# Attention on one core: q and k projected three groups ahead of their scores, the next row's normalisation moved by one step

## The chip, the cores and the metric

The kernel runs on one core of a Trainium2 chip. The metric is the device time of one execution in microseconds, the median of several runs. TensorE is called PE here, VectorE DVE, ScalarE ACT, GpSimd POOL, and SyncE, which issues all DMA transfers of this kernel, SP.

## The reference

Two layers are applied in turn to x (16 rows of the batch, 512 tokens, 512 features, float32). The change touches the first layer alone, up to its attention output y:

```python
xn = layer_norm(x, norm_w, norm_b)
q = (xn @ q_w + q_b).reshape(Bx, Tx, H, -1)
k = (xn @ k_w + k_b).reshape(Bx, Tx, H, -1)
att = jnp.einsum('bnhl,bmhl->bnmh', q, k)
att = att + (1.0 - mask) * -1000000.0
att = jax.nn.softmax(att, axis=2)
v = ((xn @ v_w + v_b) * src_mask[:, :, None]).reshape(Bx, Tx, H, -1)
y = jnp.einsum('bnmh,bmhl->bnhl', att, v).reshape(Bx, Tx, Dx)
```

There are 16 heads of 32 features. The rest of the first layer (a second normalisation, scale and shift from the conditioning vector, silu, output projection) and the whole second layer run in a second phase, which the change leaves as it is.

## The kernel before

The program has two phases, `attention_phase` and `projection_phase`, with a barrier between them. In the attention phase each of the five engines has its own instruction stream, and all order between engines is written out with semaphores.

**Groups and steps.** The 16 heads of a row of the batch are worked on in four groups (`g`, 0 to 3) of four heads. The program of every engine is a sequence of steps, one for each row `b` and group `g`, and each step has 16 slots (`k`, 0 to 15). Rows 1 to 14 run in a hardware loop, the first and the last are written out. In slot `k` of step (b, g) PE computes one exponential product (`exp_scores`, line 512) for the current group, three slots behind the step (`LAG = 3`), so slots 0 to 2 belong to the last three of the group before. In slots 0 to 10 it also computes one or two maximum products (`max_scores`, L497) for the next group, 16 in all (`maxima(k)`: slot 0 has score 0, slot 1 scores 1 and 2, slot 2 score 3, slot 3 scores 4 and 5, and so on). DVE reduces each (L862), which frees its bank; there are two banks, so score m waits until maximum m - 2 is done. In slot 12 the 16 columns of maxima are transposed (`transpose_max`, L503), DVE splits them into a high and a low part (L873, L875), and SP copies both as two rows, the shift, into `q_stack` (L325), where the exponential products of the next step need them from slot 3 on. ACT takes the exponentials (L728). PE multiplies probabilities and values after exponential products 6, 10, 14 and 2 of the next group (`weigh_values`, L523); POOL adds the probabilities of the four token tiles in three additions (`add_probs`, L271), and PE sums these after exponential product 7 of the next group (L537).

**Projections.** A projection of q, k or v is twelve products (L480) into one of two work banks, cut into four quarters of three products, each placed in a slot. `QUARTERS` names the slots: q in 0 to 3, k in 4 to 7, v tiles in 8 to 11 and 13 to 15. q and k are projected for the group two steps ahead. ACT writes the high part of the result to a staging buffer, one for q and one for k (L708), DVE the low part (L848), and SP copies them into `q_stack` and `k_stack` in three transfers each (`stack`, L318). The copies, with that of the mask rows (L310), count on one semaphore for each group, `stack_in`; PE waits for it before maximum product 0 of the group, ACT before it overwrites a staging buffer. v tiles 2 and 3 of a row are projected in step 0, tiles 0 and 1 of the next row in step 3.

**The next row.** x of row b + 1 is loaded in step 2 of the row before. Its statistics (`statistics_of_x`, L822 to L831) run on DVE in slot 13 of step 0, POOL then takes the inverse deviation (L431), and DVE normalises four tiles (L837) in slots 3 to 6 of step 1. PE transposes them in slots 8, 9, 11 and 13 (`X_TURNS`, L487), ACT and DVE write high and low parts (L702, L843), and from step 2 on the projections read the new row.

**Banks.** All uses of the two work banks are numbered in the order that `uses_of` gives, and `take_bank` makes PE wait until the use two before has been read:

```python
def take_bank(n):
    static, number = n
    if static >= 2:
        pe.wait_ge(work_read, number - 1)
    return work_bank[static % 2][:, :]
```

## Time and profile before

| | us |
|---|---|
| median of 3 runs (3141.38 to 3144.47) | 3141.91 |
| profiled execution, span on the core (no separate total of this execution is given) | 3140.1 |
| PE busy in it | 2820.6 (90%) |
| DVE, POOL, ACT busy | 1924.4, 1333.8, 1224.2 |
| attention phase, about | 1780 |

A busy share is a mean over both phases. The attention phase is the first 57% of the span and is told apart below by steps. The rows quoted later are from one row of the batch in the middle of the phase; the others repeat its pattern every 105.9 us. In the timelines a bracket behind a row is the idle time of that engine before it, and what ended it. "PEclk" is the share of full clock that TensorE was granted: 1.00 is 2.4 GHz, 0.50 is 1.2 GHz.

### The profile page before, as it was taken

To read this page: it belongs to the slowest core of one execution; us is meant where nothing else is said; L and a number is where in the kernel's file an instruction comes from. 1 tells how busy PE (TensorE), PEld (TensorE's weight loads), DVE (VectorE), ACT (ScalarE), POOL (GpSimd) and SP (SyncE) were. 2 spreads that over 40 slices of the span, in tenths; PEclk is the share of its full clock that TensorE was granted. 3 is DMA by queue.
4 is the path that set the end of the run, shared out by engine and by line. 5 is a ranking of instruction groups with operands and counts; after the bars stand their busy time and mean duration, and the time that the engine had idled before them with its cause. 6 is when DMAs were issued, how large, how long until landed. Compare 5 with 4: busy or idle time off the path is not lost. (4 is left out here: it accounts for less than half of the span.)

```text
span 3140.1 us, 43763 instructions
## 1 busy us (share of the span) xinstructions
PE 2820.6 (90%) x13890; PEld 1966.3 (63%) x13890; DVE 1924.4 (61%) x3292; ACT 1224.2 (39%) x2040; POOL 1333.8 (42%) x582
## 2 busy tenths in 40 slices
PE   6989899889988998899889789999999999999998
PEld 4555455555554555555455367777777777778876
DVE  5665666566556655665565466666666666666664
ACT  2444444444444444444444423332233333332232
POOL 0355555555555555545555333333333333333332
PEclk8999999999999999999999699999999999999999
DMA  7545454555455545545544311111101111111100
GB/s 209 93 68 85 81 85 69 85 85 85 72 85 85 85 72 85 85 72 85 85 72 72 118 48 45 44 40 44 37 34 40 40 44 44 44 42 32 43 28 27
DMA packets 114915, 211.44 MB, mean 67 GB/s; under 512 B 12408, under 2 KB 14508, under 8 KB 114876
## 3 DMA queue, kind: packets, MB, share of 16 engines
q1 hardware_dynamic: 114876, 210.94, 34.1%
q8 instruction: 22, 0.36, 0.0%
q14 instruction: 17, 0.14, 0.0%
HBM read 74.87 MB, written 34.18 MB: 35 GB/s over the span
## 5 line engine op out<-in xcount | busy, mean ns | idle before, releaser
L862 DVE TENSOR_REDUCE negmax<-max_bank 128x1 f32<-128x512 f32 x1024 | 682.6, 688 | 519.0 <-PE max_bank L497 518.6
L728 ACT ACTIVATE probs<-exp_bank 128x512 f32<-128x512 f32 x1024 | 598.3, 595 | 708.0 <-PE exp_bank L512 701.1
L271 POOL TENSOR_TENSOR probs_sum<-probs_sum,probs 128x2048 f32<-128x2048 f32 x126 | 577.4, 4582 | 224.6 <-ACT probs L728 222.8
L497 PE MATMUL max_bank<-k_stack,q_stack 98*128 98x512 f32 x1024 | 460.1, 454 | 127.1 <-DMA k_stack<-k_stage 87.8
L271 POOL TENSOR_TENSOR probs_sum<-probs 128x2048 f32<-128x2048 f32 x63 | 288.6, 4581 | 642.1 <-PE sums_bank L537 548.9
L497 PEld LDWEIGHTS max_bank<-k_stack,q_stack 98*128 98x128 f32 x1024 | 198.4, 195 | 426.7 <-issue 239.9
L512 PE MATMUL exp_bank<-q_stack,k_stack 100*128 100x512 f32 x1024 | 421.7, 423 | 23.6 <-ACT probs L728 23.3
L523 PE MATMUL y_bank<-probs,v_sb 128*32 128x512 f32 x2048 | 289.1, 638 | 0.7 <-ACT probs L728 0.7
L1487 POOL TENSOR_TENSOR sT_lo<-silu,sT_hi 128x512 fp32r<-128x512 f32 x128 | 168.1, 1324 | 238.8 <-DVE sT_hi L1602 238.8
L512 PEld LDWEIGHTS exp_bank<-q_stack,k_stack 100*128 100x128 f32 x1024 | 196.3, 195 | 109.0 <-ACT probs L728 71.8
L1269 PE MATMUL b_work<-ident,area 128*128 128x128 f32 x1536 | 195.6, 280 | 45.1 <-ACT silu L1427 18.8
L1269 PEld LDWEIGHTS b_work<-ident,area 128*128 128x128 f32 x1536 | 172.9, 144 | 65.3 <-ACT silu L1427 26.2
L1243 PE MATMUL b_work<-b_wout_hi,sT_hi 128*128 128x512 f32 x512 | 201.7, 394 | 9.6 <-issue 5.1
L1243 PE MATMUL b_work<-b_wout_lo,sT_hi 128*128 128x512 f32 x512 | 201.1, 393 | 0.0
L1243 PE MATMUL b_work<-b_wout_hi,sT_lo 128*128 128x512 f32 x512 | 201.0, 393 | 0.0
L1602 DVE CAST sT_hi<-silu 128x512 fp32r<-128x512 f32 x128 | 109.4, 865 | 113.1 <-ACT silu L1427 113.1
L1482 POOL TENSOR_TENSOR rstd_y<-var_eps_y,b_minus_half 128x4 f32<-128x4 f32 x32 | 32.7, 1022 | 322.3 <-DVE var_eps_y L1566 322.3
L1502 POOL TENSOR_TENSOR result<-area,row_out 128x512 f32<-128x512 f32 x64 | 82.7, 1294 | 181.3 <-DMA out_x<-result 181.3
L1427 ACT ACTIVATE silu<-b_work,film_b,film_a 128x512 f32<-128x512 f32 x128 | 93.0, 775 | 165.2 <-PE b_work L1269 154.3
L1243 PE MATMUL b_work<-b_wv_hi,x1T_hi 128*128 128x512 f32 x256 | 112.2, 438 | 49.7 <-ACT silu L1427 49.7
L1466 ACT ACTIVATE area<-area 128x512 f32<-128x512 f32 x64 | 40.5, 632 | 290.5 <-POOL area L1532 290.5
L1453 ACT ACTIVATE area<-area,kmax 128x512 f32<-128x512 f32 x64 | 46.3, 724 | 239.5 <-DVE kmax L1628 239.3
(203 smaller groups left out, 5397.3 us busy)
## 6 DMA issues: line engine op xcount, KB each, us to landing
q_stack<-q_stage SPq DMA_DIRECT2D x192, 256.0 KB
k_stack<-k_stage SPq DMA_DIRECT2D x192, 256.0 KB
x_sb<-in_x SPq DMA_DIRECT2D x16, 1024.0 KB, 5.4
yT_scratch<-y_stage SPq DMA_DIRECT2D x64, 256.0 KB
area<-yT_scratch SPq DMA_DIRECT2D x16, 1024.0 KB, 5.2
area<-in_x SPq DMA_DIRECT2D x64, 256.0 KB, 2.7
out_x<-result SPq DMA_DIRECT2D x64, 256.0 KB, 2.0
mask_bias<-mask_bias_scratch SPq DMA_DIRECT2D x16, 256.0 KB, 3.3
```

What stands on the lines that cost most here:

```text
L271: eng.tensor_tensor(probs_sum[:, :, :], so_far, probs[:, mt, :, :], ALU.add).then_inc(probs_added, 1)
L497: pe.matmul(max_bank[m % 2][:, :], q_stack[0:ROWS_MAX, g, j, nt * P:(nt + 1) * P], k_stack[0:ROWS_MAX, g, j, :], start=True, stop=True).th ...
L512: pe.matmul(exp_bank[k % 2][:, :], k_stack[0:ROWS_EXP, g, j, mt * P:(mt + 1) * P], q_stack[0:ROWS_EXP, g, j, :], start=True, stop=True).th ...
L523: last = pe.matmul(y_bank[DH0 * j:DH0 * (j + 1), :], v_sb[:, mt, P * j + DH0 * g:P * j + DH0 * (g + 1)], probs[:, mt, j, :], start=(mt == ...
L728: act.activation(probs[:, mt, j, :], exp_bank[k % 2][:, :], ACT.Exp).then_inc(exp_done, 1)
L862: dve.tensor_reduce(negmax[:, m:m + 1], max_bank[m % 2][:, :], AXX, ALU.max, negate=True).then_inc(max_done, 1)
L1243: last = pe.matmul(out, lhs(a, kt), rhs(c, kt), start=(kt == 0 and a + c == 0), stop=(kt == KT - 1 and a == 1))
L1269: last = pe.transpose(out[:, i * P:(i + 1) * P], src(i), ident[:, :])
L1427: act.activation(silu[:, kt % SILUS, :], bank(u), ACT.Silu, scale=film_columns(film_a[film], kt, row), bias=film_columns(film_b[film], kt, ...
L1487: pool.tensor_tensor(sT_lo[:, kt, :], silu[:, kt % SILUS, :], sT_hi[:, kt, :].bitcast(F32), ALU.subtract).then_inc(sT_lo_done, 1)
L1502: pool.tensor_tensor(result[:, tt, :], x_sb[:, tt, :], rows["out1"][:, :], ALU.add).then_inc(result_biased, 1)
L1602: dve.tensor_copy(sT_hi[:, kt, :], silu[:, kt % SILUS, :]).then_inc(sT_hi_done, 1)
```

## The change

q and k are projected three groups ahead (`AHEAD`). A table `TURNS` now gives each step its own slots: in step 0 v tiles 2 and 3 come first, then q and k; in step 1 the transposes of x come in slots 1, 3, 5, 7 and q and k in 8 to 15; in step 2 q lies in slots 4 to 7 and k in 8 to 11; step 3 is as before, but for the group after. The statistics of the next row move from slot 13 of step 0 to slot 2, the normalisation from slots 3 to 6 of step 1 to slots 9 to 12 of step 0. POOL takes the inverse deviation ahead of its first addition of step 0 instead of behind its second. q and k copies have a semaphore each, and SP issues its transfers in another order in steps 0 to 2. The prologue projects three groups of q and k instead of two. The reordering of `uses_of` follows from the table. The core of the diff:

```diff
@@ -205,34 +205,38 @@
...
+        AHEAD = 3
...
+        TURNS = [
...
+            {"v2": (0, 1, 2, 3), "v3": (4, 5, 6, 7), "q": (8, 9, 10, 11), "k": (13, 14, 15, 15)},
...
+        X_TURNS = (1, 3, 5, 7)
...
-        QUARTERS = {"q": (0, 1, 2, 3), "k": (4, 5, 6, 7), "v": (8, 9, 10, 11), "v'": (13, 14, 15, 15)}
...
-        X_TURNS = (8, 9, 11, 13)
...
@@ -356,31 +364,44 @@
             shift_rows(0, 0, FIRST_USES.index("m") + 1)
             def step(b, g, last=False, first=False):
-                if not last or g < NG - 2:
-                    s_b, s_g = (b, g + 2) if g + 2 < NG else (b + 1, g + 2 - NG)
-                    if not (first and g + 2 < NG):
-                        sp.wait_ge(exp_full, SLOTS * (step_of(b, g) - 1))
+                more = projects(g, last)
+                s_b, s_g = ahead(b, g, AHEAD)
+                def stack_of(n):
+                    sp.wait_ge(work_read, use(b, g, n, last)[1] + 1)
+                    stack(n, s_g)
+                def shift_of_next():
+                    if not last or g < NG - 1:
+                        shift_rows(*ahead(b, g, 1), use(b, g, "m", last)[1] + 1)
+                if more:
+                    if not (first and g == 0):
+                        sp.wait_ge(exp_full, SLOTS * step_of(b, g))
                     mask_rows(s_b, s_g)
                 if g == 2 and not last:
                     sp.wait_ge(work_full, use(b, 1, f"x{TT - 1}")[1] + 1)
                     if not (type(b) is int and b + 2 >= B):
                         load_x(b + 2)
-                if not last or g < NG - 2:
-                    sp.wait_ge(work_read, use(b, g, "q", last)[1] + 1)
-                    stack("q", s_g)
+                if more and g == NG - 1:
+                    stack_of("q")
                 if not (first and g == 0):
                     store_y(b, g - 1) if g else store_y(b - 1, NG - 1)
-                if not last or g < NG - 2:
-                    sp.wait_ge(work_read, use(b, g, "k", last)[1] + 1)
-                    stack("k", s_g)
+                if more and g >= 2:
+                    stack_of("q" if g == 2 else "k")
                 if g == 0 and not first:
                     store_sums(b - 1)
-                if not last or g < NG - 1:
-                    n_b, n_g = (b, g + 1) if g + 1 < NG else (b + 1, 0)
-                    shift_rows(n_b, n_g, use(b, g, "m", last)[1] + 1)
+                if g != 2:
+                    shift_of_next()
+                if more and g < 2:
+                    stack_of("q")
+                if more and g < NG - 1:
+                    stack_of("k")
+                if g == 2:
+                    shift_of_next()
             def load_x(b):
                 sp.dma_start(x_sb[:, :, :], x[b].rearrange("(t p) d -> p t d", p=P)).then_inc(x_in, DMA)
@@ -434,10 +455,10 @@
                 s = step_of(b, g)
                 if last and g == NG - 1:
                     return
+                if g == 0 and not last:
+                    inverse_deviation(b + 1)
                 add_probs(pool, s, 1, first)
                 add_probs(pool, s, 2)
-                if g == 0 and not last:
-                    inverse_deviation(b + 1)
                 add_probs(pool, s, 3)
             inverse_deviation(0)
@@ -491,7 +512,8 @@
                 j, nt = m // TT, m % TT
                 if m == 0:
-                    pe.wait_ge(stack_in[g], DMA * STACK_DMAS * (b + 1))
+                    for n in "qk":
+                        pe.wait_ge(stack_in[n][g], DMA * STACK_DMAS[n] * (b + 1))
                 if not (first and m < 2):
                     pe.wait_ge(max_done, SLOTS * step_of(b, g) + m - 1)
                 pe.matmul(max_bank[m % 2][:, :], q_stack[0:ROWS_MAX, g, j, nt * P:(nt + 1) * P],
@@ -655,24 +679,16 @@
                             max_scores(n_b, n_g, m)
                         if k == MAX_TURN:
                             transpose_max(n_b, n_g, use(b, g, "m", last))
-                    for name, slots in QUARTERS.items():
-                        if name in "qk":
-                            if last and g >= NG - 2:
-                                continue
-                            what, tile, u = name, (g + 2) % NG, name
-                        elif g == 0 or (g == NG - 1 and not last):
-                            tile = (2 if g == 0 else 0) + (name == "v'")
-                            what, u = "v", f"v{tile}"
-                        else:
-                            continue
+                    for name, slots in turns_of(g, last).items():
+                        what, tile = (name, (g + AHEAD) % NG) if name in "qk" else ("v", int(name[1]))
                         for kt in range(KT):
                             if slots[kt] != k:
                                 continue
-                            if name == "q" and kt == 0 and g == 2:
+                            if kt == 0:
+                                banks[name] = take_bank(use(b, g, name, last))
+                            if name == "q" and kt == 0 and g == 1:
                                 pe.wait_ge(work_read, use(b, 1, f"x{TT - 1}")[1] + 1)
-                            if kt == 0:
-                                banks[name] = take_bank(use(b, g, u, last))
                             project_quarter(what, tile, banks[name], kt, kt == 0, kt == KT - 1)
                     if g == 1 and not last and k in X_TURNS:
                         tt = X_TURNS.index(k)
@@ -759,10 +775,10 @@
             high_of_w("k")
             act.wait_ge(bias_done, 2)
             n = TT
-            for g in range(2):
+            for g in FIRST_GROUPS:
                 for what in "qk":
-                    if g == 1:
-                        act.wait_ge(stack_in[0], DMA * STACK_DMAS)
+                    if g:
+                        act.wait_ge(stack_in[what][g - 1], DMA * STACK_DMAS[what])
                     high_of(what, g, n, n)
                     n += 1
             copy_film(0)
@@ -987,37 +1005,43 @@
             HIGHS = 2 * NG + TT
-            def high_count(b, g, i):
-                return TT + 4 + HIGHS * b + (2 * g + (TT if g > 1 else 0)) + i + 1
+            def high_count(b, g, what):
+                before = 2 * g + (TT if g > 1 else 0)
+                at = ([f"x{tt}" for tt in range(TT)] if g == 1 else []) + ["q", "k"]
+                return TT + 2 * AHEAD + HIGHS * b + before + at.index(what) + 1
             def step(b, g, last=False):
                 has_next = not last or g < NG - 1
-                n_b, n_g = (b, g + 1) if g + 1 < NG else (b + 1, 0)
+                n_b, n_g = ahead(b, g, 1)
                 for k in range(SLOTS):
                     if has_next:
                         for m in maxima(k):
                             maximum(n_b, n_g, m)
-                    for i, what in enumerate("qk"):
-                        if k == QUARTERS[what][-1] + 1 and (not last or g < NG - 2):
-                            low_of(what, (g + 2) % NG, use(b, g, what, last)[0], high_count(b, g, i))
-                    if g == 1 and not last and 3 <= k < 3 + TT:
-                        normalise_x(b + 1, [k - 3])
+                    for what in "qk":
+                        if k == TURNS[g][what][-1] + 1 and projects(g, last):
+                            low_of(what, (g + AHEAD) % NG, use(b, g, what, last)[0], high_count(b, g, what))
+                    if g == 0 and not last and k == 2:
+                        statistics_of_x(b + 1)
+                    if g == 0 and not last and 9 <= k < 9 + TT:
+                        normalise_x(b + 1, [k - 9])
                     if g == 1 and not last and k - 1 in X_TURNS:
                         tt = X_TURNS.index(k - 1)
-                        low_of_x(tt, use(b, 1, f"x{tt}")[0], high_count(b, 1, 2 + tt))
-                    if k == 11 and (g == 0 or (g == NG - 1 and not last)):
-                        mt = 2 if g == 0 else 0
-                        add_value_bias(b if g == 0 else b + 1, mt, *use(b, g, f"v{mt}", last))
+                        low_of_x(tt, use(b, 1, f"x{tt}")[0], high_count(b, 1, f"x{tt}"))
+                    if g == 0 and k in (4, 8):
+                        mt = 2 if k == 4 else 3
+                        add_value_bias(b, mt, *use(b, 0, f"v{mt}", last))
+                    if g == NG - 1 and not last and k == 12:
+                        add_value_bias(b + 1, 0, *use(b, g, "v0"))
                     if has_next and k == MAX_TURN:
                         split_shift(n_b, n_g, *use(b, g, "m", last))
-                    if g == 0 and not last and k == 13:
-                        statistics_of_x(b + 1)
-                        if type(b) is int and b == 0:
-                            finish_film()
-                if g == 0 or (g == NG - 1 and not last):
-                    mt = 3 if g == 0 else 1
-                    add_value_bias(b if g == 0 else b + 1, mt, *use(b, g, f"v{mt}", last))
+                    if g == 0 and not last and k == 13 and type(b) is int and b == 0:
+                        finish_film()
+                for what in "qk":
+                    if TURNS[g][what][-1] == SLOTS - 1 and projects(g, last):
+                        low_of(what, (g + AHEAD) % NG, use(b, g, what, last)[0], high_count(b, g, what))
+                if g == NG - 1 and not last:
+                    add_value_bias(b + 1, 1, *use(b, g, "v1"))
             for g in range(NG):
                 step(0, g)
```

How the instructions move is shown at three places, from the written-out first row, whose order the loop repeats.

The first is DVE in step 0 of the first row, from its first reduces on, before (L857 adds the bias to a v tile, L822 to L831 are the statistics, L873 and L875 split the shift):

```order
L848 SCALAR_TENSOR_TENSOR q_stage<-work_bank,bias_cols,q_stage 128x512 [waits hi_done]
L862 TENSOR_REDUCE negmax<-max_bank 128x1 [waits max_full] x6
L848 SCALAR_TENSOR_TENSOR k_stage<-work_bank,bias_cols,k_stage 128x512 [waits hi_done]
L862 TENSOR_REDUCE negmax<-max_bank 128x1 [waits max_full] x3
L857 TENSOR_TENSOR v_sb<-work_bank,v_bias 128x512 [waits work_full]
L873 CAST shift<-work_bank 16x128 [waits shift_in0,work_full]
L875 TENSOR_TENSOR shift<-work_bank,shift 16x128 [waits shift_hi]
L822 BN_STATS stats<-x_sb 128x6 [waits x_in]
L822 BN_STATS stats<-x_sb 128x6 x3
L826 MEMSET var_eps 128x4 [waits ln_stats]
L828 BN_AGGR mv<-stats 128x2 x4
L831 TENSOR_TENSOR var_eps<-mv,var_eps 128x4 [waits ln_stats]
```

And the same place now:

```order
L879 TENSOR_REDUCE negmax<-max_bank 128x1 [waits max_full] x4
L839 BN_STATS stats<-x_sb 128x6 [waits x_in]
L839 BN_STATS stats<-x_sb 128x6 x3
L843 MEMSET var_eps 128x4 [waits ln_stats]
L845 BN_AGGR mv<-stats 128x2 x4
L848 TENSOR_TENSOR var_eps<-mv,var_eps 128x4 [waits ln_stats]
L879 TENSOR_REDUCE negmax<-max_bank 128x1 [waits max_full] x3
L874 TENSOR_TENSOR v_sb<-work_bank,v_bias 128x512 [waits work_full]
L879 TENSOR_REDUCE negmax<-max_bank 128x1 [waits max_full] x6
L874 TENSOR_TENSOR v_sb<-work_bank,v_bias 128x512 [waits work_full]
```

The statistics have moved from behind the last reduce to behind the fourth, with twelve reduces and both v tiles after them.

The second is the normalisation (L837) before, on DVE in step 1, behind the first six reduces:

```order
L862 TENSOR_REDUCE negmax<-max_bank 128x1 [waits max_full] x6
L837 TENSOR_SCALAR x_sb<-x_sb,mv,rstd 128x512 [waits rstd_done]
L862 TENSOR_REDUCE negmax<-max_bank 128x1 [waits max_full]
L848 SCALAR_TENSOR_TENSOR q_stage<-work_bank,bias_cols,q_stage 128x512 [waits hi_done]
L837 TENSOR_SCALAR x_sb<-x_sb,mv,rstd 128x512 [waits rstd_done]
L862 TENSOR_REDUCE negmax<-max_bank 128x1 [waits max_full] x2
L837 TENSOR_SCALAR x_sb<-x_sb,mv,rstd 128x512 [waits rstd_done]
L862 TENSOR_REDUCE negmax<-max_bank 128x1 [waits max_full]
```

And now, where it is L854, at the end of step 0:

```order
L879 TENSOR_REDUCE negmax<-max_bank 128x1 [waits max_full] x2
L854 TENSOR_SCALAR x_sb<-x_sb,mv,rstd 128x512 [waits rstd_done]
L879 TENSOR_REDUCE negmax<-max_bank 128x1 [waits max_full]
L854 TENSOR_SCALAR x_sb<-x_sb,mv,rstd 128x512 [waits rstd_done] x2
L865 SCALAR_TENSOR_TENSOR q_stage<-work_bank,bias_cols,q_stage 128x512 [waits hi_done]
L854 TENSOR_SCALAR x_sb<-x_sb,mv,rstd 128x512 [waits rstd_done]
L890 CAST shift<-work_bank 16x128 [waits shift_in0,work_full]
L892 TENSOR_TENSOR shift<-work_bank,shift 16x128 [waits shift_hi]
```

Three of the four tiles have moved ahead of, and one behind, the low part of q, and all four ahead of the shift.

The third is SP in step 2 before (mask rows, the load of x, q copies, the store of y, k copies, shift):

```order
L310 DMA k_stack<-mask_bias_scratch 2x4x512 [waits exp_full]
L386 DMA x_sb<-in_x 128x4x512 [waits work_full]
L318 DMA q_stack<-q_stage 32x4x512 [waits work_read]
L318 DMA q_stack<-q_stage 32x4x512 x2
L391 DMA yT_scratch<-y_stage 4x32x512 [waits y_read]
L318 DMA k_stack<-k_stage 32x4x512 [waits work_read]
L318 DMA k_stack<-k_stage 32x4x512 x2
L325 DMA q_stack<-shift 1x16x128 [waits work_read]
L325 DMA q_stack<-shift 1x16x128
```

And now:

```order
L318 DMA k_stack<-mask_bias_scratch 2x4x512 [waits exp_full]
L407 DMA x_sb<-in_x 128x4x512 [waits work_full]
L412 DMA yT_scratch<-y_stage 4x32x512 [waits y_read]
L326 DMA q_stack<-q_stage 32x4x512 [waits work_read]
L326 DMA q_stack<-q_stage 32x4x512 x2
L326 DMA k_stack<-k_stage 32x4x512 [waits work_read]
L326 DMA k_stack<-k_stage 32x4x512 x2
L333 DMA q_stack<-shift 1x16x128 [waits work_read]
L333 DMA q_stack<-shift 1x16x128
```

The store of y has moved ahead of the q copies; k copies and shift stand as before, while k itself is now finished four slots later.

## Rows read from the trace of the kernel before

**Rows 1.** Windows of steps 0 to 3: us, busy by engine, PEclk, DMA, GB/s.
```profile
724.60:749.50 24.90, 24.87 (x122) 15.69 (x122) 17.42 (x32) 12.72 (x22) 13.62 (x4) 1.00 0.50 76
...
749.50:777.40 27.90, 24.14 (x114) 13.44 (x113) 22.41 (x30) 13.51 (x24) 13.64 (x5) 0.94 0.44 67
...
777.40:803.60 26.20, 20.16 (x98) 11.00 (x97) 12.47 (x20) 11.58 (x20) 17.28 (x4) 0.95 0.59 112
...
803.60:830.50 26.90, 26.89 (x121) 16.18 (x121) 13.25 (x22) 11.32 (x19) 11.49 (x4) 0.93 0.46 69
```

**Rows 2.** Waits of PE, 698 to 804 us: in total, times, longest.
```profile
PE max_bank L497 <- DMA k_stack<-k_stage: 9.4, 3, 4.1
...
PE max_bank L497 <- DVE negmax L862: 2.3, 3, 1.0
...
PE exp_bank L512 <- ACT probs L728: 1.4, 3, 0.7
```

**Rows 3.** Timeline of PE, start and us: stalls in steps 1 and 3.
```profile
763.14 0.71 PE L497 MATMUL max_bank<-k_stack,q_stack 98*128 98x512 f32 x1 [0.98 <-DVE negmax L862]
...
803.61 0.79 PE L497 MATMUL max_bank<-k_stack,q_stack 98*128 98x512 f32 x1 [4.14 <-DMA k_stack<-k_stage]
```

**Rows 4.** SP's issues in step 2, and the landing time of the shift copies.
```profile
793.27 1.87 SPq L318 DMA_DIRECT2D k_stack<-k_stage  x3
...
797.01 1.21 SPq L325 DMA_DIRECT2D q_stack<-shift  x2
...
q_stack<-shift SPq DMA_DIRECT2D x2, 8.0 KB, 5.5
```

**Rows 5.** Timelines of DVE, POOL and PE, slots 2 to 4 of step 0.
```profile
728.47 1.29 DVE L862 TENSOR_REDUCE negmax<-max_bank 128x1 f32<-128x512 f32 x2 [0.24 <-PE max_bank L497]
...
729.46 4.61 POOL L271 TENSOR_TENSOR probs_sum<-probs_sum,probs 128x2048 f32<-128x2048 f32 x1 [1.99 <-ACT probs L728]
...
731.08 0.40 PE L497 MATMUL max_bank<-k_stack,q_stack 98*128 98x512 f32 x1
...
731.32 0.40 PE L480 MATMUL work_bank<-xT_hi,wk_hi 128*128 128x512 f32 x1
```

**Rows 6.** Statistics and normalisation before, with POOL's addition; var_eps as a group.
```profile
745.67 0.67 DVE L822 BATCH_NORM_STATS2 stats<-x_sb 128x6 f32<-128x512 f32 x1
...
748.58 4.02 DVE L831 TENSOR_TENSOR var_eps<-mv,var_eps 128x4 f32<-128x4 f32 x1
...
747.97 4.60 POOL L271 TENSOR_TENSOR probs_sum<-probs_sum,probs 128x2048 f32<-128x2048 f32 x1 [0.84 <-ACT probs L728]
...
758.08 2.70 DVE L837 TENSOR_SCALAR x_sb<-x_sb,mv,rstd 128x512 f32<-128x512 f32 x1
...
L831 DVE TENSOR_TENSOR var_eps<-mv,var_eps 128x4 f32<-128x4 f32 x14 | 56.2, 4018 | 0.5
```

**Rows 7.** POOL and PE in slots 10 to 13 of step 0.
```profile
742.52 4.61 POOL L271 TENSOR_TENSOR probs_sum<-probs 128x2048 f32<-128x2048 f32 x1 [8.45 <-PE sums_bank L537]
...
745.97 0.50 PE L480 MATMUL work_bank<-wv_hi,xT_hi 128*128 128x512 f32 x1
```

**Rows 8.** Groups of DVE, 200 to 1700 us: the reduces of the maxima.
```profile
L862 DVE TENSOR_REDUCE negmax<-max_bank 128x1 f32<-128x512 f32 x906 | 604.3, 688 | 455.4 <-PE max_bank L497 455.4
```

**Rows 9.** Timeline of PE where x is transposed in step 1.
```profile
768.37 1.06 PE L523 MATMUL y_bank<-probs,v_sb 128*32 128x512 f32 x8
...
769.36 0.50 PE L497 MATMUL max_bank<-k_stack,q_stack 98*128 98x512 f32 x1
...
769.70 0.60 PE L487 MATMUL work_bank<-ident,x_sb 128*128 128x128 f32 x4
...
770.06 0.48 PE L497 MATMUL max_bank<-k_stack,q_stack 98*128 98x512 f32 x1
```

**Rows 10.** Timeline of ACT in the prologue: the second group's q.
```profile
54.20 0.69 ACT L708 ACTIVATE q_stage<-work_bank,bias_cols 128x512 fp32r<-128x512 f32 x1 [15.35 <-DMA k_stack<-k_stage]
```

**Rows 11.** Window of step 2 of the last row, columns as in rows 1.
```profile
1727.00:1746.00 19.00, 19.00 (x53) 7.30 (x57) 10.06 (x15) 6.38 (x11) 5.12 (x2) 0.50 0.06 15
```

84 lines of the change are left out of this document (43 added, 41 removed), and 3 rows, old and new, of the table TURNS.

## The prediction

> **What bounds the kernel.** I read the views in this order: windows by step, waits, the timelines of PE where it stalls, then those of DVE, POOL and SP at the places to which the change moves work. The projection phase behind the attention phase is untouched. In the attention phase one row of the batch takes 105.9 us, the sum of its four steps. PE has work in 96.06 us of them and none in 9.84; DVE, the next busiest, has 65.6 [rows 1]. So PE sets the pace, and only its stalls and its clock can change. Of the 9.84 us, 5.3 are two waits for the copies into the stacks (the view gives 9.4 for three, of which one of 4.1 belongs to the row before), 2.3 are waits for maxima and 1.4 for exponentials [rows 2]. The wait of 4.14 us stands at the start of step 3 [rows 3].
>
> A stall also costs clock. Steps 0 and 3 hold the same kinds and numbers of products, but step 3 starts behind the long wait and takes 26.90 us at a mean clock of 0.93, where step 0 takes 24.90 at 1.00 [rows 1]. That is 2.0 us. A second slow stretch follows the wait of 0.98 us in step 1 (clock 0.94) [rows 1, 3]. I price a slow stretch, at 1.2 GHz in place of 2.4, at 1.8 us beyond its stall, a little under the 2.0 since the second stall is the shorter. Before, a batch row has two: 3.6 us. Loss before: 9.84 + 3.6 = 13.44 us a row.
>
> **What goes.** Both waits for copies go. A k copy whose three issues begin at 793.27 had landed when PE went on at 803.61, 10.3 us later [rows 3, 4]. Now its scores follow a whole step (25 us) later still, so more than 10 us are spare. The moved statistics and normalisation take their old stalls (the DVE waits of step 1) along. A third of the waits for exponentials, 0.45 us at the end of step 2, I keep.
>
> **A, the statistics at slot 2 of step 0.** DVE now does maxima 0 to 3, then the statistics, then maximum 4. The reduce of maximum 3 ends at 728.47 + 1.29 = 729.76. The operation on var_eps started 2.91 us after the first of the statistics (745.67 to 748.58), so it would start at 732.6 [rows 5, 6]. But it does not run beside POOL's addition: its mean is 4.02 us for four elements a partition, 14 times over, and in the row shown it ended at 752.60, POOL's addition at 752.57 [rows 6]. The addition of the last probabilities of the step before runs from 729.46 to 734.07 [rows 5], so DVE is held until then. Maximum 4, another 0.69 us [rows 8], ends at 734.75. PE's score 6 uses the bank that maximum 4 frees, and PE wants it at 731.08 [rows 5]. Stall 3.7 us, then a slow stretch. Without the hold it would be 2.2 us.
>
> Here a page speaks against the change. The Trainium skill, "SBUF — State Buffer", section "Who interferes with whom", says that a VectorE operation with two SBUF inputs, or in a two-port mode (tensor_scalar can be), waits until a GpSimd operation that reads SBUF is through, and that tensor_reduce never does. By that rule the port hurts at exactly the two edits A and B and nowhere else; without it the sum would be rival 1's. The trace agrees: 4.02 us on var_eps, 0.69 on every reduce.
>
> **B, the normalisation at slots 9 to 12 of step 0.** A tile that met an addition took 2.70 us [rows 6]. Tile 0 (slot 9) is free. Tile 1 follows maximum 15 in slot 10, and POOL's first addition starts at 742.52, right after the product for the sums, and ends at 747.13 [rows 7]; the tile ends near 747.4. Tile 2 and the low part of q bring DVE to 748.5. The first quarter of k (slot 13) needs the bank of q and has the place of a product that ran at 745.97 [rows 7]. Stall 2.6 us. I add half a slow stretch, since the stall lies between one that cost none and the 4.14 that did.
>
> **C, slots 0 to 8 of step 1.** Here DVE must first do the low part of k (behind ACT's high part, two operations of some 0.7 us, so maximum 0 starts 1.4 us in), then 13 maxima and 4 low parts of x before PE may start q, which waits for the last x. Two reduces in a row take 1.29 us [rows 5], so 0.63 is the pace: 17 x 0.63 + 1.4 = 12.1, with gaps 12.4 us. PE's own work there is 9 exponential and 13 maximum products at 0.24, two groups of value products at 1.0 and 0.1 on either side, four transposes of x at 0.36 [rows 5, 9]: 5.3 + 2.4 + 1.4 = 9.1. Stall 3.3 us, and a slow stretch.
>
> **D, slots 0 to 4 of step 2.** No quarter lies between the maxima now. DVE starts 1.4 us in and needs 0.63 for each; score 6 needs maximum 4, at 1.4 + 5 x 0.63 = 4.6, and later still through the banks, against some 3.5 of PE's work. Stall 1.1 us. The empty slots before were 8 to 15, where most maxima are done.
>
> **E, the shift row of step 2.** SP issues it right behind the k copies, where k is now finished in slot 12. A shift issued at 797.01, 3.7 us behind the first k copy, landed 5.5 us later, so 9.2 after that first k copy [rows 4]. The exponential of slot 3 in step 3 wants it some 6.4 us after k's first issue: four slots without quarters (3.6 us, my estimate) and three with quarters (4.8, as 724.6 to 729.4 in step 0), less the 2.0 us that ACT, DVE and SP take with k. The bounds are 0 (the small copy overtakes) and 9.2 - 6.4 = 2.8 us; I take 1.3, below the middle, as the y store no longer lies between q and k.
>
> **Prologue and last row.** The third q and k are projected before the first film products, one staging buffer each, and ACT's copy waits for the copies before: 15.35 us for the second group already [rows 10]. A third round adds about one landing; I take 9.7 us (10.3 us less what overlaps; bounds 4 and 14). The last row loses two projections on PE, 24 products at 0.24, 5.6 us; but a step without quarters behind a stall ran 19 us at clock 0.50 with PE busy throughout [rows 11]. I take back 2. Net +7.7.
>
> All else is neutral: the counts of products, maxima and copies are the same; the split of the semaphores adds one wait instruction per step on PE. Moving SP's q and k copies behind the shift and the sums in step 0 and 1 delays only copies with 10 us spare. POOL's rstd now comes ahead of its first addition, near 734.3, where POOL is idle until 742.5 [rows 7].
>
> **The sum.** After: 3.7 + 2.6 + 3.3 + 1.1 + 0.45 + 1.3 = 12.45 us of stalls, 2.5 slow stretches = 4.5, together 16.95 against 13.44: +3.5 us a row, times 15 rows with a normalisation = 52; with 7.7: +60. The profiled execution spans 3140.1 us, the median of three runs is 3141.9; the sum is made on the span, and I carry the 1.8 us over: 3141.9 + 60 = 3202.
>
> **Rivals.**
> 1. *The gain of the copies prevails.* The mechanism is the order in which DVE and POOL reach the port: if the var_eps operation and the tile come ahead of the additions, A is 2.2 and B 0, with two slow stretches: 2.2 + 3.3 + 1.1 + 0.45 + 1.3 + 3.6 = 11.95, so -1.5 a row, -22 + 7.7: 3127 us, faster. For it: the additions wait for exponentials and sums, whose times shift. Against it: the last exponential of a step releases the addition while DVE is still at maximum 3 (729.46 and 729.76) [rows 5]. It decides once the additions start more than 3.1 us later relative to DVE (732.6 - 729.46).
> 2. *The stalls come, the clock holds.* Only A costs clock, E is nothing: 11.15 + 1.8 = 12.95, -0.5 a row, -7 + 7.7, in all 3142: no change. For it: step 2 loses 6.0 us to waits (26.20 less 20.16) and shows 0.95, so the waits before its last cost little clock [rows 1]. Against: 0.98 us were enough in step 1 [rows 3].
> 3. *The clock stays low.* Slots 0 to 8 of step 1 now have no quarters; behind B the engine may keep 1.2 GHz through them, as it did for 19 us in the last row [rows 11]. Then PE's 9.1 us there become about 16, another 3.6 us a row: 3254.
>
> **Chances.** Forecast (3165 to 3235) 0.55; rival 3 0.17; rival 2 0.12, spread evenly about no change; rival 1 0.16. The range leaves out part of rivals 1 and 3: 3122 to 3252. No change means within 0.2%, 6.3 us, about what a measurement of this kernel can tell: 0.06. Faster takes rival 1 and part of 2: 0.20. Slower: 0.74.
>
> **What would show it.** No wait of PE for copies between rows; a PE wait near 3.7 us for a maximum four scores into step 0; one near 2.6 us for q's low part in slot 13; one for x's low part in slot 8 of step 1; var_eps near 1.5 us and one tile near 4. The forecast is wrong if PE passes slot 4 of step 0 without a wait, or if its busy time per row falls by more than its stalls grow.

## The result and the profile after

The changed kernel takes 3229.4 us (median of four runs, 3227.1 to 3236.8) beside 3143.2 us (3141.4 to 3145.3) for the kernel before on the same chip: 1.0277 times, 95% interval 1.0262 to 1.0291, so 86 us slower. The forecast was 3202 us, with a range of 3122 to 3252.

The head of the page after. PE's busy share went from 90 to 89%, yet PE is busy 52 us longer (2820.6 before) with the same 13890 products:

```profile
span 3228.9 us, 43808 instructions
...
PE 2872.4 (89%) x13890; PEld 1982.0 (61%) x13890; DVE 1900.7 (59%) x3292; ACT 1226.8 (38%) x2040; POOL 1333.6 (41%) x582
```

Windows of steps 0 to 3 of row 6 after, the columns of [rows 1]:

```profile
770.10:804.33 34.23, 28.27 (x122) 17.16 (x122) 22.95 (x36) 12.85 (x23) 16.33 (x5) 0.90 0.09 19
804.33:830.46 26.13, 23.95 (x114) 12.76 (x114) 14.74 (x24) 12.99 (x23) 12.20 (x4) 0.93 0.46 65
830.46:851.70 21.24, 20.55 (x98) 10.71 (x97) 13.12 (x21) 11.38 (x20) 12.41 (x4) 1.00 1.03 167
851.70:882.76 31.06, 27.54 (x122) 17.20 (x122) 13.25 (x21) 12.07 (x21) 15.05 (x4) 0.89 0.58 85
```

Step 0 went from 24.90 to 34.23 us, step 1 from 27.90 to 26.13, step 2 from 26.20 to 21.24, step 3 from 26.90 to 31.06 [rows 1]. Step 2, in which both waits for copies lay before, and step 1 got shorter, the other two got longer by more: 112.7 us for this row against 105.9. Its busy time rose by 4.25 us (96.06 to 100.31) and its idle time by 2.5 (9.84 to 12.35), with the same number of products in steps 0 to 2 and one more in the window of step 3.

The same holds over the fifteen rows with a normalisation. The window from step 0 of row 0 to step 0 of row 15, of the kernel before and of the kernel after:

```profile
87.03:1676.84 1589.81, 1440.95 (x6775) 847.34 (x6771) 983.92 (x1539) 736.27 (x1272) 832.62 (x194) 0.95 0.50 81
```

```profile
98.42:1776.58 1678.16, 1494.96 (x6775) 865.98 (x6772) 960.53 (x1539) 738.48 (x1272) 832.26 (x194) 0.93 0.49 76
```

The stretch grew by 88.4 us, 5.9 a row. Idle time (length less PE busy) grew from 148.9 to 183.2, by 34.3; busy time grew by 54.0 with 6775 products in both, at a mean clock of 0.93 for 0.95. **More of the loss is clock than waiting.** Row 0 also starts 11.4 us later, the last row is 11.9 us shorter, the projection phase 1.0 longer: 88.4 + 11.4 - 11.9 + 1.0 = 88.9, the 88.8 between the spans.

Waits of PE in that window after (in total, times, longest):

```profile
PE max_bank L519 <- DVE negmax L879: 65.1, 60, 3.5
PE exp_bank L534 <- DMA q_stack<-shift: 51.2, 15, 3.8
PE work_bank L501 <- DVE q_stage L865: 38.5, 15, 3.4
PE work_bank L501 <- DVE xT_lo L860: 20.8, 15, 1.5
PE exp_bank L534 <- ACT probs L744: 6.7, 15, 0.5
```

and before, in its own window:

```profile
PE max_bank L497 <- DMA k_stack<-k_stage: 79.5, 31, 4.4
PE max_bank L497 <- DVE negmax L862: 35.0, 45, 2.1
PE exp_bank L512 <- ACT probs L728: 20.7, 44, 0.7
```

The waits for k's copies (79.5 us, two a row) are gone, as intended. In their place stand four that come once a row: for a maximum (3.5 at the longest, before 2.1), for q's low part and for the shift (neither was there before), and for x's low part (1.5; before 0.6). Where they stand, timeline of PE after:

```profile
780.09 0.62 PE L519 MATMUL max_bank<-k_stack,q_stack 98*128 98x512 f32 x1 [3.44 <-DVE negmax L879]
...
799.21 0.50 PE L501 MATMUL work_bank<-xT_hi,wk_hi 128*128 128x512 f32 x1 [2.51 <-DVE q_stage L865]
...
816.98 0.50 PE L501 MATMUL work_bank<-xT_hi,wq_hi 128*128 128x512 f32 x1 [1.38 <-DVE xT_lo L860]
...
860.17 0.79 PE L534 MATMUL exp_bank<-q_stack,k_stack 100*128 100x512 f32 x1 [3.52 <-DMA q_stack<-shift]
```

**The first two** stand behind DVE operations that met POOL's additions. Timelines of DVE and POOL after, at slot 2 and at slots 10 to 12 of step 0:

```profile
778.00 1.43 DVE L848 TENSOR_TENSOR var_eps<-mv,var_eps 128x4 f32<-128x4 f32 x1
779.35 2.09 DVE L879 TENSOR_REDUCE negmax<-max_bank 128x1 f32<-128x512 f32 x3
...
774.87 4.54 POOL L279 TENSOR_TENSOR probs_sum<-probs_sum,probs 128x2048 f32<-128x2048 f32 x1 [1.69 <-ACT probs L744]
...
792.41 0.54 DVE L854 TENSOR_SCALAR x_sb<-x_sb,mv,rstd 128x512 f32<-128x512 f32 x1
...
794.08 4.42 DVE L854 TENSOR_SCALAR x_sb<-x_sb,mv,rstd 128x512 f32<-128x512 f32 x2
798.42 0.74 DVE L865 SCALAR_TENSOR_TENSOR q_stage<-work_bank,bias_cols,q_stage 128x512 fp32r<-128x512 f32 x1
...
793.18 4.58 POOL L279 TENSOR_TENSOR probs_sum<-probs 128x2048 f32<-128x2048 f32 x1 [12.56 <-PE sums_bank L559]
```

POOL's first addition ends at 779.41, var_eps (four elements a partition) at 779.43; the three reduces behind it are late. Tile 0 of x is normalised in 0.54 us with POOL idle, tiles 1 and 2 start at 794.08 and end at 798.50, POOL's addition ends at 797.76 (tile 1 alone takes 3.96 us). Just ahead of them, at 793.47, a reduce beside the same addition took its usual 0.69 us.

**The fourth** is SP's queue. SP in steps 2 and 3 after, and then the landing time of the shift copies issued from 850 to 862 us:

```profile
831.97 1.85 SPq L326 DMA_DIRECT2D k_stack<-k_stage  x3
...
834.58 0.42 SPq L407 DMA_DIRECT2D x_sb<-in_x  x1
838.49 0.64 SPq L412 DMA_DIRECT2D yT_scratch<-y_stage  x1
843.59 2.15 SPq L326 DMA_DIRECT2D q_stack<-q_stage  x3
850.17 1.85 SPq L326 DMA_DIRECT2D k_stack<-k_stage  x3
852.13 1.22 SPq L333 DMA_DIRECT2D q_stack<-shift  x2
```

```profile
q_stack<-shift SPq DMA_DIRECT2D x2, 8.0 KB, 6.7
```

Nine copies of 256 KB, the load of x (1 MB) and the store of y are issued within 20 us. The DMA engines are full in step 2 (share 1.03, where before it was 0.59 [rows 1]), the load of x lands in a median of 12.7 us (5.4 before) and the shift's 8 KB in 6.7 (5.5 before [rows 4]). PE went on at 860.17, 10.0 us after the first of the k copies.

**The clock.** Four stretches of this row run partly at the lower of the two levels (0.50, 1.2 GHz in place of 2.4), and so it is in twelve of the fifteen rows; in the row shown before, two did. Windows of 4 us in row 6 after, one in each:

```profile
778.00:782.00 4.00, 1.92 (x5) 1.32 (x5) 3.88 (x5) 0.00 (x0) 2.43 (x2) 0.79 0.00 0
800.00:804.00 4.00, 4.00 (x12) 3.15 (x11) 0.12 (x1) 1.20 (x2) 2.78 (x1) 0.60 0.36 74
817.00:821.00 4.00, 4.00 (x14) 1.63 (x15) 0.04 (x1) 0.60 (x1) 0.00 (x0) 0.61 0.05 21
860.00:864.00 4.00, 3.83 (x9) 3.06 (x10) 1.39 (x3) 1.72 (x3) 0.99 (x1) 0.50 0.00 0
```

Each follows one of the four stalls above; in the second and third PE was busy all of the 4 us, and slow. But a stall does not always bring one. A later row of the same execution has the same stalls (3.4, 3.5, 2.5 and 1.4 us at the longest) and only two slow stretches, and PE is busy 3 us less in it than in the next:

```profile
1172.47:1281.99 109.52, 97.22 (x452) 56.24 (x452) 64.03 (x103) 49.29 (x86) 56.00 (x14) 0.95 0.51 78
1281.99:1394.51 112.52, 100.29 (x452) 57.88 (x452) 64.04 (x103) 49.30 (x86) 55.96 (x14) 0.92 0.49 76
```

**The prologue.** ACT after, the third group's q and k: each waits for the copies of the group before it.

```profile
60.79 0.69 ACT L724 ACTIVATE q_stage<-work_bank,bias_cols 128x512 fp32r<-128x512 f32 x1 [4.62 <-DMA q_stack<-q_stage]
...
66.08 0.69 ACT L724 ACTIVATE k_stage<-work_bank,bias_cols 128x512 fp32r<-128x512 f32 x1 [4.60 <-DMA k_stack<-k_stage]
```

The rounds follow each other by 5.3 us (55.48, 60.79, 66.08), two more of them are 10.6 of the 11.4 us.

### The profile page after: what moved, and what is told of

Read it like the earlier page. It is cut to its first block and busy times, and to the rows that moved or that the text cites. A ratio compares the mean times of both kernels' runs of the same rounds, so it can differ in the third digit from the quotient of the medians.

```text
span 3228.9 us, 43808 instructions
## 1 busy us (share of the span) xinstructions
PE 2872.4 (89%) x13890; PEld 1982.0 (61%) x13890; DVE 1900.7 (59%) x3292; ACT 1226.8 (38%) x2040; POOL 1333.6 (41%) x582
## 5 line engine op out<-in xcount | busy, mean ns | idle before, releaser
L519 PE MATMUL max_bank<-k_stack,q_stack 98*128 98x512 f32 x1024 | 477.5, 468 | 74.4 <-DVE negmax L879 73.3
L534 PE MATMUL exp_bank<-q_stack,k_stack 100*128 100x512 f32 x1024 | 430.1, 429 | 60.5 <-DMA q_stack<-shift 51.2
L534 PEld LDWEIGHTS exp_bank<-q_stack,k_stack 100*128 100x128 f32 x1024 | 204.5, 200 | 145.5 <-DMA q_stack<-shift 57.8
L501 PE MATMUL work_bank<-xT_hi,wk_hi 128*128 128x512 f32 x256 | 114.7, 448 | 38.9 <-DVE q_stage L865 38.8
## 6 DMA issues: line engine op xcount, KB each, us to landing
x_sb<-in_x SPq DMA_DIRECT2D x16, 1024.0 KB, 12.7
```

Of the source, the lines that this page charges most:

```text
L501: last = pe.matmul(out, lhs, rhs, start=(first and i == 0), stop=(stop and i == 2))
L519: pe.matmul(max_bank[m % 2][:, :], q_stack[0:ROWS_MAX, g, j, nt * P:(nt + 1) * P], k_stack[0:ROWS_MAX, g, j, :], start=True, stop=True).th ...
L534: pe.matmul(exp_bank[k % 2][:, :], k_stack[0:ROWS_EXP, g, j, mt * P:(mt + 1) * P], q_stack[0:ROWS_EXP, g, j, :], start=True, stop=True).th ...
```

## The experiments

The theory was that of the prediction: the wait removed is real, but statistics and tiles now lie where POOL's additions hold DVE (A, B), and the shift lies behind k's copies (E); each stall also costs clock. The rivals were that POOL or the queue is not the cause (then the edit moves a stall elsewhere), and that going three groups ahead is itself what costs.

### E alone: the shift ahead of k's copies

```diff
+                if g == 2:
+                    shift_of_next()
                 if more and g < NG - 1:
                     stack_of("k")
-                if g == 2:
-                    shift_of_next()
```

> The changed kernel, but in step 2 SP issues the shift ahead of the k copies. My theory: the wait of 3.4 us for the shift in step 3 goes, and with it a slow stretch of the clock of about 2 us, so 5.4 us a row of the batch, 15 rows, about 80 us less than the changed kernel: 3150 us. Rival: the shift waits behind the copies of q and the load of x that are in flight anyway; then under 20 us are gained (over 3210 us).

Measured 3154.1 us, 1.004 times before (1.0026 to 1.0054): 75 us less than after. The wait for the shift (51.2 us) is gone from the profile, and nothing waits for the k copies, which now follow it. A shift issued at 818.50 in step 2 landed in 3.4 us there, where it had taken 6.7. That lies in the order of the three k copies and the shift: the load of x still lands in 12.7 us. Two rows of it, one behind the other:

```profile
693.41:802.40 108.99, 100.18 (x452) 58.07 (x452) 63.95 (x103) 49.12 (x86) 56.05 (x14) 0.92 0.51 78
802.40:908.40 106.00, 97.19 (x452) 56.63 (x452) 63.94 (x103) 49.08 (x86) 56.06 (x14) 0.95 0.52 81
```

51 us are the stall, the other 24 are clock (PE is busy 26.6 us less in all, 2845.8 for 2872.4). From the second row on its rows come in such pairs, 109.0 and 106.0 us in turn, with the same stalls: in the first kind a third stretch goes slow, behind the wait for x's low part, and the one behind q's low part lasts some 7 us instead of 4; in the second kind neither happens.

### A alone: the statistics in step 3, one tile a slot

Statistics of row b + 2 in slots 5 to 8 of step 3, var_eps in slot 9, the inverse deviation on POOL ahead of that step's first addition; those of row 1 stay in slot 2 of step 0 of the first row. The tiles stay in slots 9 to 12 of step 0.

```diff
-                    if g == 0 and not last and k == 2:
-                        statistics_of_x(b + 1)
+                    if g == NG - 1 and not last and not (type(b) is int and b + 2 >= B):
+                        if 5 <= k < 5 + TT:
+                            statistics_of_tile(b + 2, k - 5)
+                        if k == 9:
+                            finish_statistics(b + 2)
```

> The changed kernel, but the statistics of the row after next run in step 3, one tile a slot in slots 5 to 8 and the rest in slot 9, where POOL is idle; the normalisation stays in slots 9 to 12 of step 0. My theory: the wait of 3.45 us at score 6 of step 0 goes, with a slow stretch of about 2 us; 5.4 us in 14 rows, 75 us less: 3155 us. Rival: DVE is short of time over the whole row, so the stall turns up in step 3 instead, and less than 25 us are gained (over 3204 us).

Measured 3180.9 us, 1.0131 (1.0103 to 1.0159): 48.5 less than after, not 75. The waits for maxima (100 to 1850 us) fell from 67 us, with 3.5 the longest, to

```profile
PE max_bank L523 <- DVE negmax L890: 24.0, 67, 2.6
```

so the stall at slot 2 is gone and the wait removed is about the whole gain. In step 3 no addition runs beside var_eps, and the same operation takes 0.16 us, where it took 1.43 in the changed kernel and 4.02 before (DVE, 200 to 1700 us):

```profile
L859 DVE TENSOR_TENSOR var_eps<-mv,var_eps 128x4 f32<-128x4 f32 x13 | 2.1, 164 | 0.4
```

That prices the hold at slot 2: 1.3 of the 3.44 us. The rest is what the statistics take of DVE between two maxima (the forecast had 2.2), and the edit moves both away; no run separates them by time. Hardly any clock came back (PE busy 2864.5 us for 2872.4), where a slow stretch a row, 27 us, had been expected. A row of this kernel:

```profile
699.96:809.17 109.21, 100.08 (x452) 58.24 (x452) 62.50 (x103) 49.24 (x86) 55.92 (x14) 0.92 0.51 78
```

Cut into windows of 2 us it shows three slow stretches instead of four, but longer ones: PE is busy 100.08 us, as after.

### A and B: the tiles in slots 6 to 9 as well

The edit above, and

```diff
-                    if g == 0 and not last and 9 <= k < 9 + TT:
-                        normalise_x(b + 1, [k - 9])
+                    if g == 0 and not last and 6 <= k < 6 + TT:
+                        normalise_x(b + 1, [k - 6])
```

The slots lie before the product for the sums releases POOL's next addition.

> As stats_early, and the four tiles are normalised in slots 6 to 9 of step 0, between two of POOL's additions. My theory: the wait of 2.5 us for q's low part in slot 13 goes too, with a slow stretch: 4.4 us in 15 rows, 66 us less than stats_early, about 3090 us. Rival: the late start of slot 13 is made by ACT's and DVE's work on q itself, not by the held tile; then no more than 15 us come off stats_early.

Measured 3094.3 us, 0.9852 (0.9836 to 0.9869), 87 less than the kernel above and 135 less than after. The wait for q's low part fell from 38.7 to 5.2 us (0.4 the longest). Every tile now takes 0.54 us, so the stall of slot 13 was the hold:

```profile
L865 DVE TENSOR_SCALAR x_sb<-x_sb,mv,rstd 128x512 f32<-128x512 f32 x56 | 30.2, 538 | 0.0
```

A row has one slow stretch, behind the wait for the shift:

```profile
668.99:771.79 102.80, 95.73 (x452) 55.76 (x452) 59.09 (x103) 49.26 (x86) 56.03 (x14) 0.97 0.54 83
```

Of the 87 us, 33.5 are wait removed and most of the rest is clock given back: PE is busy 62.7 us less (2864.5 and 2801.8) in profiled executions that lie 92 us apart. A and B together are worth 135 us where my prices gave 141; singly they were far off (48.5 and 87). Waits add up, slow stretches do not belong to a stall each.

### The other half alone: the statistics and tiles moved, two groups ahead

The kernel before, with the statistics in slot 2 of step 0, the tiles in slots 9 to 12 and POOL's inverse deviation ahead of its additions.

```diff
-                    if g == 1 and not last and 3 <= k < 3 + TT:
-                        normalise_x(b + 1, [k - 3])
+                    if g == 0 and not last and k == 2:
+                        statistics_of_x(b + 1)
+                    if g == 0 and not last and 9 <= k < 9 + TT:
+                        normalise_x(b + 1, [k - 9])
```

> The kernel before, with one part of the change alone: statistics in slot 2 of step 0, normalisation in slots 9 to 12 of step 0, POOL's inverse deviation ahead of its first addition; q and k still two groups ahead. My theory: stalls of 3.7 and 2.6 us and two slow stretches (3.8 us) come, the old stalls of step 1 (2.5 us and a slow stretch of 1.8) go: +5.8 us a row, 15 rows, about 3230 us, as slow as the whole change. Rival: what costs is the third group ahead (thin slots, a late start of DVE, the copies), and the moved statistics are neutral: 3143 us within 15.

Measured 3235.4 us, 1.0298 (1.028 to 1.0315): 93 slower than before (3142.2 in those runs), all of the change's loss and without its third group. The time is the one expected, but a part of it is luck: the wait for copies, taken as unchanged, grew by 19 us (83.6 before). Its waits show both the old and the new:

```profile
PE max_bank L497 <- DMA k_stack<-k_stage: 102.7, 31, 4.4
PE max_bank L497 <- DVE negmax L862: 48.8, 16, 3.5
PE work_bank L480 <- DVE v_sb L857: 37.5, 15, 3.3
```

Adding the third group (that is the changed kernel) brings 3229.4, so at this placement going three ahead is worth some 6 us, no more than the measurements tell apart. The wait for copies it removes (102.7) comes back as the shift's 51, 18 more for maxima (66.8), 13 more for x's low part (20.8 for 8.2), the prologue's 11, and PE busy 30 us longer (2872.4 for 2842.6).

### Both mends together

The edits of the first and of the third experiment in one kernel:

```diff
                 if g == 2:
                     shift_of_next()
...
+                    if g == NG - 1 and not last and not (type(b) is int and b + 2 >= B):
...
+                    if g == 0 and not last and 6 <= k < 6 + TT:
```

> tiles_early and shift_first together. If the stalls are independent, as my theory has it, their gains add: tiles_early measured 3094 us, the shift 75 us (3229 to 3154), so about 3019 us. Rival: the stalls share slow stretches of the clock or cover each other, and the shift is worth less than half here: over 3057 us.

Measured 3019.3 us, 0.9612 (0.9596 to 0.9628). The two gains, 75 and 135, add to within a microsecond.

### Does it need the third group at all?

The kernel before, with the statistics and tiles where A and B put them; two groups ahead.

```diff
-                    if g == 1 and not last and 3 <= k < 3 + TT:
-                        normalise_x(b + 1, [k - 3])
+                    if g == NG - 1 and not last and not (type(b) is int and b + 2 >= B):
...
+                    if g == 0 and not last and 6 <= k < 6 + TT:
+                        normalise_x(b + 1, [k - 6])
```

> The kernel before, two groups ahead, but with statistics and normalisation where tiles_early has them. My theory: the old stalls of step 1 go (2.5 us and a slow stretch of 1.8), the waits for copies and their slow stretch stay: 4.3 us in 15 rows, 64 us less than before, about 3078 us; against both, the third group ahead would then be worth some 60 us. Rival: PE only reaches the copies earlier and waits longer there: gains under 30 us, over 3112 us.

Measured 3137.5 us (ten runs), 0.9987 (0.9978 to 0.9997). My theory said 3078; the rival held. The waits for maxima fell from 35.0 us to 7.3, but those for copies rose (100 to 1850 us; before 83.6):

```profile
PE max_bank L501 <- DMA k_stack<-k_stage: 102.1, 31, 4.4
PE exp_bank L516 <- ACT probs L732: 20.1, 36, 0.7
...
PE max_bank L501 <- DVE negmax L873: 7.3, 17, 1.9
```

With two groups ahead the copies are what ends last, so PE that arrives earlier waits longer for them. The clock took the rest: a row in the middle waits 0.9 us less than before (9.0 and 9.8) but is busy 0.8 longer (96.9 and 96.1), as the waits for copies are now 2.5 and 4.2 us long (1.1 and 4.1 before), and a slow stretch of some 7 us follows the shorter one too. With three ahead the same placement gives 3094, and with the shift mended 3019. **The two halves need each other.** The better placement alone takes 4 us off the kernel before, the third group with the shift first but at the change's placement adds 12 (3154.1), both take 123 off. Against the change's placement the better one is worth 98 us with two ahead (3235.4 to 3137.5) and 135 with three; the third group, with the shift first, is worth 81 at the change's placement (3235.4 to 3154.1) and 118 at the better one (3137.5 to 3019.3). So each is worth 37 us more beside the other.

### C: q in step 1 one slot later

PE waits for x's low part at the first quarter of q in slot 8. In the mended kernel:

```diff
-            {"q": (8, 9, 10, 11), "k": (13, 14, 15, 15)},
+            {"q": (9, 10, 11, 11), "k": (13, 14, 15, 15)},
```

> As both, but q in step 1 starts in slot 9 (quarters in 9, 10, 11, 11) instead of 8. The wait of 1.4 us for x's low part ahead of q should go, since PE has 1.9 us of other products first, and if the clock follows stalls, part of a slow stretch: 1.4 to 3.2 us in 15 rows, 20 to 48 us less than both. Rival: q's low part is then late for the first quarter of k in slot 13 and the wait only moves: within 8 us of both.

Measured 2976.6 us, 0.9477 (0.9461 to 0.9493), 43 less. The wait (20.8 us) is gone, and with it the last slow stretch, which every other row of the kernel without this edit still had (98.1 and 96.6 us in turn). Rows 1 to 14 now run at full clock:

```profile
724.38:819.30 94.92, 92.73 (x452) 54.36 (x452) 59.00 (x103) 49.19 (x86) 56.13 (x14) 1.00 0.58 90
```

This row prices the others: its 452 products take 92.7 us at full clock, so the clock cost 96.06 - 92.7 = 3.4 us a row before and 100.3 - 92.7 = 7.6 after.

### The prologue

The third group is projected between the first maximum products, behind the film products.

```diff
-            for g in FIRST_GROUPS[1:]:
-                for what in "qk":
-                    project(what, g, n)
-                    n += 1
+            for what in "qk":
+                project(what, 1, n)
+                n += 1
...
+                if m in (4, 8):
+                    project("q" if m == 4 else "k", 2, n)
+                    n += 1
```

> As both, and in the prologue the third group of q and k is projected between the first maximum products, behind the film products, ACT's film copies and the split of wv, instead of ahead of them. My theory: 11.4 us were lost in the prologue by waits for staging buffers; 7 of them come back, 7 us less than both. Rival: the prologue's PE chain is bound elsewhere, the projections only move: within 3 us of both.

Measured 3023.1 us, 0.9625 (0.9609 to 0.9641), 4 more than without the edit, not 7 less, and a little outside what the rival allowed (3). The stall moved: SP issues the second film weights behind the third group's copies, which now come later, and PE waits for them:

```profile
97.74 1.06 PE L581 MATMUL sums_bank<-x_sb,condT 128*32 128x512 f32 x2 [11.05 <-DMA probs<-in_L_cond_W_emb]
```

So the load goes ahead of those copies in SP's order, on top of q one slot later; its partner ran again beside it.

```diff
             for g in FIRST_GROUPS:
+                if g == 2:
+                    sp.wait_ge(film_full, 1)
+                    sp.wait_ge(w_split, 3)
+                    sp.wait_ge(bias_made, 3)
+                    for part in range(4):
+                        load_emb(1, part)
                 for i, n in enumerate("qk"):
```

> both_q_later with the prologue of both_prologue (third group projected between the first maxima) and, new, SP issuing the second load of film weights ahead of the third group's copies. If the 11 us wait of PE for the film weights in both_prologue came from the place of that load in SP's queue, it goes, and the three quarters of the prologue's loss remain as gain: both_q_later less 4 to 9 us, 2970 us. Rival: the third group's copies and the weights compete for the same DMA engines, so the order is indifferent and the prologue stays level or 4 us slower: 2977 to 2981 us.

> both_q_later again, on the same chip, as the partner of the run with the changed prologue: 2976.6 us within 3 us if nothing but the chip differs.

Measured 2971.3 us, 0.9459 (0.9443 to 0.9475), against 2979.2, 0.9484 (0.9468 to 0.95): the wait for film weights is gone, and the medians differ by 8 us as expected, though the two intervals overlap a little. The longest wait that PE still has in this prologue:

```profile
55.57 1.19 PE L524 MATMUL max_bank<-k_stack,q_stack 98*128 98x512 f32 x2 [6.53 <-DMA k_stack<-k_stage]
```

This is the best version: 169 us less than the kernel before it (3140.2 us in those runs) and 258 less than the change.

## Why the prediction was right in kind and short in size

Slower was forecast, with 0.74, and it came: +86 us where +60 stood. By the steps of the prediction, per row:

| step | forecast, us | measured, us | from |
|---|---|---|---|
| waits for copies | gone | gone | no such wait in the list |
| A, statistics at slot 2 | 3.7 | 3.44 | 780.09 |
| B, tiles at slots 9 to 12 | 2.6 | 2.57 | 38.5 / 15 |
| C, slots 0 to 8 of step 1 | 3.3 | 2.17 | 0.39 + 0.40 + 1.38 |
| D, slots 0 to 4 of step 2 | 1.1 | 0.18 | 834.63 |
| exponentials | 0.45 | 0.45 | 851.40 |
| E, the shift | 1.3 | 3.41 | 51.2 / 15 |
| sum of stalls | 12.45 | 12.2 | 183.2 / 15 |
| clock | 4.5 | 7.6 | 100.3 - 92.7 |

**What goes** was right: both waits for copies vanished, and with 10 us to spare nothing late took their place at that semaphore. **A and B** were right in place, size and cause; var_eps ended within 0.02 us of POOL's addition, and a tile was held to its end. The Trainium skill, "SBUF — State Buffer", section "Who interferes with whom", says that a VectorE operation with two SBUF inputs, or a tensor_scalar in a two-port mode, contends with a GpSimd operation that reads SBUF, and that tensor_reduce never does. The trace agrees: clear of the additions var_eps takes 0.16 us and a tile 0.54, beside them 1.43 and 3.96, and a reduce 0.69 in either place. The experiment that moved both operations clear of the additions took 135 us off, with the same instructions on every engine; a part of A's share of it is the place of the statistics and not the hold. Rival 1 (the additions come later than the DVE operations) did not occur: the addition started 3.1 us ahead of var_eps (774.87 and 778.00), as it had been reckoned, 729.46 and 732.6.

**C and D** were too high. DVE's side was right: q could start 12.6 us into step 1 (804.37 to 816.98), 12.4 reckoned, and in step 2 seven reduces took 4.61 us from 1.4 us on. PE's side was the term mis-sized: it had 12.6 - 2.17 = 10.4 us of work of its own ahead of q where I counted 9.1, and in step 2 enough to wait 0.18 us only. Yet the 1.38 for x's low part, once removed, was worth 43 us with its clock.

**E** was the worst of the terms: 1.3 taken, bounds 0 and 2.8, measured 3.4. The moment at which PE wants the row was right (6.5 us after k's first issue; 6.4 reckoned). The arrival was not: 10.0 us after that issue, where 9.2 was my upper end. The step that failed is "I take 1.3, below the middle, as the y store no longer lies between q and k": I looked at the queue between q and k, and not at what stands ahead of it. The k copies of step 1 and the load of x now fall into the same 20 us, and the DMA share of step 2 went from 0.59 to 1.03.

**The clock** was the step that failed in the sum. That the sum of stalls came out right (12.45 against 12.2 us) is luck: E's excess and C's and D's shortfall cancel. The stalls grew by 34 us over the rows, where 2.6 x 15 = 39 stood. Busy time grew by 54 us where 0.9 x 15 = 14 stood. I had priced 2.5 slow stretches at 1.8 us; there are four, at 7.6 / 4 = 1.9 in row 6. In this row the mean price was right and the number wrong; in other kernels the price was not (3.0 for the single one of A and B mended). I gave A and C one each, B a half and E none; in fact B's stall of 2.51 us and E's of 3.52 brought one each too, and C's did so with 1.38. Rival 3 (half clock right through slots 0 to 8 of step 1) is not it: steps 1 and 2 show 0.93 and 1.00. (By its own terms rival 3 comes to 3202 + 54 = 3256 us, not 3254; nothing hangs on it.) Rival 2, that the clock holds, is refuted by the 54 us of busy time.

**Prologue and last row.** 9.7 forecast, 11.4 measured: two rounds of 5.3 and a little. The last row gave 11.9 back where I took 2. Step 2 of it ran at 1.00, not at the 0.50 of [rows 11]. The window begins 2 us into step 2 and reaches into step 3:

```profile
1821.00:1842.00 21.00, 18.68 (x86) 6.68 (x85) 10.26 (x17) 12.53 (x23) 17.04 (x5) 1.00 0.05 14
```

The 24 products were worth their 5.6 us after all, and some 3 us each came with the clock and with shorter waits (PE busy 9 us less, idle 3 less over the last row). I had reasoned that a slow stretch would eat the gain, since the row of before showed one there; but the wait for copies that stood ahead of it had gone with the change.

In all, 60 = 39 + 14 + 9.7 - 2 was forecast and 88.8 = 34.3 + 54.0 + 11.4 - 11.9 + 1.0 measured: 40 us too little for the clock, 5 too much for the stalls, and 10 too little taken back in the last row.

What stays open is what sets the number and length of slow stretches: why the clock gave next to nothing back when A alone was mended, more than the wait when B followed, and why rows with equal stalls alternate where E alone, A and B, or all three are mended. No run here separates that.

## What to carry to other kernels

When a transfer is taken off the path by working further ahead, look at where the work that had to move lands: here an operation on four elements a partition beside a long POOL addition, and 8 KB behind 3.6 MB of other copies, gave back more than the wait removed, while the third group with those placed well (and C and the prologue mended) takes 5.4% off. Move short DVE operations on SBUF into slots in which POOL waits, and issue the small transfer that somebody needs next ahead of large ones that have a step to spare. Compare busy time at equal numbers of products to see what the clock took, and give it a range of its own: here from 0.5 to 4.2 us a row for the removal of a stall of 2.5 to 3.5.

## What the runs showed of the hardware beyond that

- A stall's price in clock is not fixed. A wait for the shift of 3.48 us cost the row 95.7 - 92.7 = 3.0 us of clock when it was the only long one, and one of 3.44 in the row ahead of it 94.75 - 92.7 = 2.0; the removal of a stall of 3.44 (A alone) gave back 7.9 / 15 = 0.5, and that of 2.5 (B next) 62.7 / 15 = 4.2.
- One stall of 1.4 us was enough for a slow stretch, but not every time: in the alternating rows of the first experiment the same stall (1.4 us both times) brought one in every other row. With it gone from the kernel with A, B and E mended, rows 1 to 14 ran at full clock and the kernel was 43 us shorter for 21 us of wait.
- The load of 1 MB of x lands in a median of 5.4 us in the kernel before, where the last copies of 256 KB were issued from 7.7 us ahead of it (769.30 and 776.98), and in 12.7 in the changed one, where six were issued from 5.9 and 2.6 us ahead (828.72, 831.97 and 834.58), without harm here, since x is wanted a row later.
